# A two-layer kernel: rounded passes for two products, a moved weight product, an earlier Tanh and a moved tile step

## What is computed

```python
xn = layernorm(x)
# layer 0: a small state-space branch and a gated feed-forward with ternary weights
h  = silu(conv(xn @ in_w.T + in_b) + conv_b)
a, b = exp(-exp(xp[:16])), silu(xp[16:]) * h.sum()        # xp = h @ xp_w.T + xp_b
s_t = s_{t-1} * a_t + b_t                                  # scan over the sequence
u  = silu((xn @ w1.T) * w1_s) * ((xn @ w2.T) * w2_s)       # 128 -> 512, twice
u  = gelu((u @ h1.T) * h1_s); u = gelu((u @ h2.T) * h2_s)  # 512 -> 512
x  = x + (s @ out_w.T + out_b) + (u @ w3.T) * w3_s
# layer 1: test-time-training attention, and a mixture of 8 experts (top 2) with a shared expert
xn = layernorm(x)
# attention: 16 heads of 64, chunks of 64 tokens; per chunk
#   Z = K W + b, normalised; gradient of the loss; W -= (eta K)^T grad; out = norm(Q W + b)
# experts: scores = sigmoid(xn @ gate_w.T + gate_b), top 2, y = w2_e(gelu(w1_e x)); shared expert on all tokens
x  = x + attention(xn) @ wo + routed + 0.1 * shared
```

## Time and profile before

| | |
|---|---|
| median of 3 runs | 624.35 us (621.68 to 625.32) |
| the profiled execution | 628.44 us, span 626.6 us |
| mean granted clock of TensorE | 0.965 |
| TensorE busy (matmul / weight load) | 92% / 67% of the span |
| VectorE, ScalarE, GpSimd busy | 77%, 50%, 43% |
| first layer | 0 to about 195 us |
| second layer, chunks of one block | about 98 us for a block |

### The profile page before, as it was taken

One profiled execution on the slowest core, in us unless ns is written; L12 is line 12 of the kernel. 1 busy time (PEld: TensorE's weight loads), 2 busy tenths in 40 slices (PEclk: granted clock), 3 DMA queues, 4 the chain that ended last, 5 costly groups with the idle time before them and its releaser, 6 DMA issues.

```text
span 626.6 us, 14164 instructions
## 1 busy us (share of the span) xinstructions
PE 576.5 (92%) x5515; PEld 418.2 (67%) x5515; DVE 485.3 (77%) x866; ACT 315.0 (50%) x598; POOL 267.8 (43%) x253
## 2 busy tenths in 40 slices
PE   2999999999998979898999999999999989998886
PEld 0477574773774635555778777878778768677576
DVE  2694787995994596898769969877869879779793
ACT  1553566583475614451656456756357566345111
POOL 0933000036066363238241844862744853616422
PEclk9999999998999889896999999999999999999598
DMA  7999300000001010004516115325203423000301
...
DMA packets 37890, 53.15 MB, mean 85 GB/s; under 512 B 10168, under 2 KB 23120, under 8 KB 37440
## 3 DMA queue, kind: packets, MB, share of 16 engines
...
## 4 chain that ended last, share of the span: by engine, by line
PE 69%; DVE 21%; POOL 4%; issue 3%; ACT 2%; DMA 0%; POOLq 0%; SPq 0%; ACTq 0%; DVEq 0%
PE ps L963 10%; PE ps L824 8%; PE ps L1066 7%; PE ps L1029 4%; PE ps L830 4%; PE ps L1132 4%; PE ps L1074 4%; PE ps L1037 4%; POOL small L687 3%; PE ps L989 3%; PE ps L1116 3%; DVE small L1832 2%; PE ps L886 2%; PE ps L936 2%; PE ps L887 2%
## 5 line engine op out<-in xcount | busy, mean ns | idle before, releaser
L687 POOL TENSOR_TENSOR small<-small 128x8 f32<-128x8 f32 x32 | 53.6, 1685 | 109.5 <-DVE small L1770 109.4
L766 POOL TENSOR_TENSOR small<-small 128x8 f32<-128x8 f32 x32 | 52.0, 1641 | 38.2 <-DVE small L1762 38.2
L731 POOL DMA_INDIRECT ys_dram<-ybuf,slot_row x39 | 51.7, 1325 | 12.8 <-issue 8.3
L1386 ACT ACTIVATE sq<-ps 128x512 f32<-128x512 f32 x32 | 19.1, 597 | 66.8 <-PE ps L1066 66.8
L1418 ACT ACTIVATE work<-ps,b1t 128x128 f32<-128x128 f32 x156 | 44.6, 369 | 15.5 <-PE ps L1029 13.3
L1116 PE MATMUL ps<-grad,l 64*64 64x64 f32 x1024 | 32.1, 227 | 13.0 <-DVE grad L1847 12.2
L1762 DVE TENSOR_REDUCE small<-sq 128x8 f32<-128x520 f32 x32 | 22.1, 694 | 27.2 <-ACT sq L1386 26.4
L1377 ACT ACTIVATE x_query<-ps 128x512 f32<-128x512 f32 x32 | 17.5, 594 | 49.7 <-PE ps L989 49.7
L1544 DVE RECIPROCAL got<-got 128x512 f32<-128x512 f32 x8 | 26.8, 3348 | 19.3 <-ACT got L1272 19.3
L1116 PEld LDWEIGHTS ps<-grad,l 64*64 64x64 f32 x1024 | 30.1, 140 | 16.8 <-issue 12.8
L715 POOL DMA_INDIRECT xs_dram<-wtile,pos x32 | 36.3, 1135 | 9.8 <-issue 7.6
...
## 6 DMA issues: line engine op xcount, KB each, us to landing
...
```

The source lines that it names most:

```text
L687: pool.tensor_tensor(small[:, 240 + 8 * p:248 + 8 * p], small[:, 224 + 8 * p:232 + 8 * p], small[:, 384:392], ALU.pow).then_inc(q_r.sem, 1)
L731: pool.indirect_dma_start(ys_dram, bass.IndirectOffsetOnAxis(ap=slot_row[:, k:k + 1], axis=0), ybuf[:, k // 4 % 2, k % 4], None).then_inc( ...
L766: pool.tensor_tensor(small[:, 16 + 8 * p:24 + 8 * p], small[:, 8 * p:8 * p + 8], small[:, 384:392], ALU.pow).then_inc(z_r.sem, 1)
```

## The change

- **w1 and w2 in three rounded passes.** For blocks 1 to 3 each float32 product with `w1` or `w2` becomes three passes on rounded parts. GpSimd splits the two weights into `wt` (free until the target weights fill it), after it has waited for `x_lo`. VectorE splits the normalised block i+1 into `xn_hi` and `xn_lo` in block i. Block 0 stays as it was. `xn_hi` lies in the memory of `sw1`, so the load of `sw1` moves behind block 3's w1 and w2 products.
- **Target weights** move from the end of block 2 to the end of block 3, with ScalarE's copies and VectorE's subtractions; TensorE's wait for them moves ahead of the first target product.
- **Tanh.** A Tanh on two numbers is done after the keys, so that the table is loaded there, and the last gates' Tanh stands ahead of the target copies.
- **Ranks** of the last block stand ahead of all shared products.
- **One tile step** goes from (2,1) to (3,2).

```diff
--- before.py
+++ after.py
@@ -113,6 +113,8 @@
         wq = sb("wq", [P, 2, NH * HD], F32R)
         wk = sb("wk", [P, 2, NH * HD], F32R)
         wt = sb("wt", [P, 2, NH * HD], F32R)
+        with ExitStack() as first_layer:
+            xn_hi = first_layer.enter_context(nc.sbuf_tensor("xn_hi", [P, NB], F32R))
         sw1 = sb("sw1", [P, HID])
         xb_s = sb("xb_s", [P, 2, NB], F32R)
         wo = sb("wo", [P, NQ, D])
@@ -142,6 +144,7 @@
         gb = got[:, 0].rearrange("p k d -> p (k d)")
         xb_t = sb("xb_t", [P, 2, NB], F32R)
         x_less = sb("x_less", [P, NB])
+        xn_lo = sb("xn_lo", [P, NB], F32R)
 
         work = sb("work", [P, 8192])
         used = [0]
@@ -272,7 +275,7 @@
         a_u = signal("a_u", KC)
         a_uh, a_ul = signal("a_uh", KC), signal("a_ul", KC)
         a_gh, a_gl = signal("a_gh", KC), signal("a_gl", KC)
-        h_sp = sem("h_sp")
+        h_sp, x_hi, x_lo = sem("h_sp"), sem("x_hi"), sem("x_lo")
         a_h1 = signal("a_h1", KC)
         a_g1 = signal("a_g1", KC)
         a_h2 = signal("a_h2", KC)
@@ -365,7 +368,7 @@
             take_slot(("out", i, 0), a_res.sem, a_res.at(i, 2))
             if i == 0:
                 take_slot(("prep", 0, 0), p_dve, 3)
-            if i == 2:
+            if i == NBLK - 1:
                 for p in range(2):
                     take_slot(("wt", 0, p), w_t, p + 1)
         slot_no = {k: n for n, (k, _, _) in enumerate(slots)}
@@ -388,7 +391,7 @@
 
         TILES = 4 * QUADS - 1
         STEPS = {(0, 3): 4, (1, 0): 5, (1, 1): 1, (1, 2): 5, (1, 3): 4,
-                 (2, 0): 5, (2, 1): 1, (2, 2): 5, (2, 3): 3, (3, 0): 5, (3, 2): 3}
+                 (2, 0): 5, (2, 2): 5, (2, 3): 3, (3, 0): 5, (3, 2): 4}
         assert sum(STEPS.values()) == TILES + 2
 
         def steps_before(i, c):
@@ -545,12 +548,14 @@
             sp.dma_start(wqT, a["wqT"]).then_inc(ld_c, 16)
             sp.dma_start(wkT, a["wkT"]).then_inc(ld_c, 16)
             sp.dma_start(sw2[:, :, :], a["mw2"][:, EXP * KC:, :]).then_inc(ld_m, 16)
-            sp.dma_start(sw1[:, :], a["mw1"][:, EXP, :]).then_inc(ld_s, 16)
             sp.wait_ge(zeroed, 1)
             sp.dma_start(xs_dram.rearrange("(p t) d -> p (t d)", p=P).rearrange("p (r z) -> p r z", z=ZEROS),
                          zeros.unsqueeze(1).to_broadcast([P, SLOTS // P * ROW // ZEROS, ZEROS])).then_inc(z_st, 16)
 
             for i in range(NBLK):
+                if i == NBLK - 1:
+                    sp.wait_ge(a_w12.sem, a_w12.at(i, KC))
+                    sp.dma_start(sw1[:, :], a["mw1"][:, EXP, :]).then_inc(ld_s, 16)
                 sp.wait_ge(a_res.sem, a_res.at(i, 2))
                 sp.dma_start(x_dram[:, blk(i)], x_sb[:, blk(i)]).then_inc(x_st[i], 16)
             sp.wait_ge(b_ctc, 1)
@@ -661,7 +666,14 @@
                 step(pool.tensor_copy(to[:, 0], src))
                 step(pool.tensor_tensor(to[:, 1], src, to[:, 0], ALU.subtract))
 
-            pool.wait_ge(a_gl.sem, a_gl.at(0, KC))
+            pool.wait_ge(ld_a, 6 * 16)
+            pool.wait_ge(x_lo, 1)
+            for n, w in enumerate((w1, w2)):
+                at = slice(n * HID, (n + 1) * HID)
+                pool.tensor_copy(wt[:, 0, at], w).then_inc(h_sp, 1)
+                parts[0] += 2
+                pool.wait_ge(h_sp, parts[0] - 1)
+                pool.tensor_tensor(wt[:, 1, at], w, wt[:, 0, at], ALU.subtract).then_inc(h_sp, 1)
             step(pool.tensor_tensor(wv_f, wk_f, wv_f, ALU.subtract))
             step(pool.tensor_tensor(gb[:, :], gg[:, :], gb[:, :], ALU.mult))
             step(pool.tensor_tensor(heads_of(wkv_f), wv_f.rearrange("p (q h d) -> p h q d", h=2, d=HD), heads_of(gg[:, :]),
@@ -882,10 +894,20 @@
                 for m in range(DC):
                     pe.matmul(open_slot("in", i, m), in_w[:, m * P:(m + 1) * P], xn[:, blk(i)],
                               start=True, stop=True).then_inc(a_in.sem, 1)
+                if i:
+                    pe.wait_ge(x_lo, i)
+                    pe.wait_ge(h_sp, 4 * KC + 4)
                 for m in range(KC):
-                    pe.matmul(open_slot("w1", i, m), w1[:, m * P:(m + 1) * P], xn[:, blk(i)], start=True, stop=True)
-                    pe.matmul(open_slot("w2", i, m), w2[:, m * P:(m + 1) * P], xn[:, blk(i)],
-                              start=True, stop=True).then_inc(a_w12.sem, 1)
+                    for n, (kind, w) in enumerate((("w1", w1), ("w2", w2))):
+                        to = open_slot(kind, i, m)
+                        if i:
+                            at = slice(n * HID + m * P, n * HID + (m + 1) * P)
+                            pe.matmul(to, wt[:, 0, at], xn_hi[:, :], start=True, stop=False)
+                            pe.matmul(to, wt[:, 1, at], xn_hi[:, :], start=False, stop=False)
+                            mm = pe.matmul(to, wt[:, 0, at], xn_lo[:, :], start=False, stop=True)
+                        else:
+                            mm = pe.matmul(to, w[:, m * P:(m + 1) * P], xn[:, blk(i)], start=True, stop=True)
+                    mm.then_inc(a_w12.sem, 1)
                 centre(*ahead_of[0])
                 if i >= 2:
                     pe.wait_ge(ln_out.sem, ln_out.at(norm_no[1, i - 2], 1))
@@ -940,13 +962,11 @@
                 pe.matmul(to, out_w, ssm[0:NST, 4], start=True, stop=True).then_inc(a_o.sem, 1)
                 if i == 0:
                     folded_weights()
-                if i == 2:
+                if i == NBLK - 1:
                     target_weights()
 
             pe.wait_ge(p_dve, PREP)
             pe.wait_ge(p_pool, P_LATE)
-            pe.wait_ge(w_t, 2)
-
 
             def free(kind, i, which):
                 n = ring_no[kind, i, which]
@@ -1165,6 +1185,7 @@
             pe.wait_ge(ln_out.sem, ln_out.at(norm_no[1, NBLK - 1], 1))
             pe.wait_ge(*last_slot[3])
             gates(bank(3), NT - JB, NT)
+            pe.wait_ge(w_t, 2)
             project_targets(0, 0)
             tokens_turned(free("x", NBLK - 1, 0), NBLK - 1).then_inc(r_pe, 1)
 
@@ -1186,9 +1207,8 @@
                 tiles(steps_of(i, 0, 0, 3))
                 project_targets(i, 1)
                 if i == 0:
-                    shared_up(0, 0, 1)
                     ranks(NBLK - 1, bank(2), 0)
-                    shared_up(0, 1, KC)
+                    shared_up(0)
                     shared_up(1, 0, 2)
                     shared_down(0)
                     shared_up(1, 2, KC)
@@ -1464,9 +1484,10 @@
             keys_in(0, 1, 3)
             spread_in(1, NBLK - 1)
             keys_in(0, 3, NQ)
+            act.activation(small[:, 100:102], eps_ln, ACT.Tanh)
             key_squares(0, 0)
+            gates_in(NBLK - 1)
             targets_in(0, 0)
-            gates_in(NBLK - 1)
             tokens_out(take("x", NBLK - 1, 0), NBLK - 1).then_inc(r_act, 1)
             for i in range(NBLK):
                 keys_by_token(i, 0)
@@ -1699,6 +1720,11 @@
                         less_hi(i, m - 1, a_gh, a_gl)
                 less_hi(i, KC - 1, a_gh, a_gl)
                 normalised(*ahead_of[0])
+                if i < NBLK - 1:
+                    dve.wait_ge(ln_out.sem, ln_out.at(norm_no[ahead_of[0]], 1))
+                    dve.tensor_copy(xn_hi[:, :], xn[:, blk(i + 1)]).then_inc(x_hi, 1)
+                    dve.wait_ge(x_hi, i + 1)
+                    tt(xn_lo[:, :], xn[:, blk(i + 1)], xn_hi[:, :], ALU.subtract).then_inc(x_lo, 1)
                 if i >= 2:
                     places(i - 2, slot_bank("rank", i - 2, 0), 0)
                 if i == NBLK - 1:
```

## The result

The changed kernel takes 616.66 us (median of 4, 613.75 to 617.28), the kernel before beside it 624.83: a ratio of 0.9872, 95% interval 0.9823 to 0.9921. It is faster by 8.2 us, more than the 5.1 forecast, and inside the range. A second set, taken with the later experiments, gave 0.9837 (0.9733 to 0.9940). The profiled execution took 616.73 us with a span of 614.9, against 628.44 and 626.6.

A forecast was written before the change was run, and what follows sets the result against it. The prediction took TensorE (69% of the chain of waits), then VectorE (21%), and TensorE's half-rate clock as bounds. Terms -2.3 + 1.1 + 0.4 - 1.9 - 0.5 - 1.9 = -5.1 us took 624.35 to 619.3, range 614.5 to 624.5.

The forecast's parts named there:

- Passes: w1 and w2 products, blocks 1 to 3: gains of 1.37, 0.9 and nothing, together -2.3 us.
- one such meeting: Block 3: a VectorE subtraction meeting GpSimd's token splitting costs up to 1.3 us, eating the 1.37 gain.
- GpSimd in block 0: Block 0: GpSimd's later weight splitting delays VectorE's scans, so TensorE gets the state output 1.1 us late; +1.1 us.
- the stepping in turns: Block 0: VectorE and GpSimd instructions taken alternately, second scan ending at 56.4, state output 1.1 us late.
- Target weights: Moved behind block 3: half-rate stretch follows to the key projections, square-root table load some 0.4 us late; +0.4 us.
- Tanh and ranks: Second layer's start: early Tanh and ranks before shared products bring the gradients forward by 1.04 + 0.86; -1.9 us.
- Step out of (2,1): Chunk (2,1): removing a 2.0 us tile step gives only -0.5 us, as turned queries then wait for ScalarE.
- Step into (3,2): Chunk (3,2): the added step fills TensorE's 3.51 us pause, so updates run at full rate; -1.9 us.
- Of the rivals, the first: Half rate retreats further, before 230 and at block 3's start, 1.6 us each: 617.7 or 616.1; chance 0.17.
- The second: VectorE takes the passes' gain and (3,2) stays at half rate: 623.5; chance of both 0.1, of one 0.2.
- The third: Slower: new short waits bring half rate into the first layer, 1.6 us per stretch, 628.9; chance 0.05.
- The fourth: The change doesn't do what it says: the Tanh table load could be issued twice; chance under 0.02.

The follow-up runs named there:

- A second set: The changed kernel, unedited, measured and profiled again beside the later experiments: 621.00 us against 629.56 for the kernel before, ratio 0.9837.
- before's second profile: The kernel before, with no edit, profiled once more: 627.66 us, span 625.8.

## Why the prediction was right, and where not

- **Passes, -2.3.** Right: 2.7 us by stages at like clock. Block 1 gave 1.30 (1.37), block 2 0.81 (0.9), block 3 0.55 (0.4 to 0.8 over the profiles) where the step said nothing; "one such meeting, up to 1.3 us, eats the 1.37" took the meeting at its upper bound, and the rows show 0.48.
- **GpSimd in block 0, +1.1.** Mis-sized: 0. From the first `in_w` product to the state output of block 0 it takes 39.35 us in the changed kernel and 39.36 in before's second profile; over all profiles it is 39.0 to 40.6 us with either code, and TensorE nowhere waits for the state output. The step that failed is the stepping in turns: it had GpSimd through its four short instructions by 51.5 and put the 2.4 us ones opposite the scans. They were held by VectorE themselves and ran to 53.67, so the scans met a cast and a subtraction, and ended at 54.2, not 56.4. The Trainium skill's rule (SBUF — State Buffer, "Who interferes with whom") is not at fault: the rows show both stretched, VectorE's and GpSimd's. The use of it here was.
- **Target weights, +0.4.** Mis-sized, and for a wrong reason. The move costs nothing (99.23 against 99.20 us). "I assume that the half-rate stretch follows its instructions" failed: it followed in one of eight profiles with the moved order fully and in two by 1.3 us. Behind block 2 and up to the key state, four of six profiles of the old order had 1.7 to 5 us of it. Over the profiles at hand, with the 1.36 us of the passes in blocks 2 and 3 added back, the mean is 101.3 us for the old order (99.2 to 104.2) and 100.2 for the new (99.0 to 103.8), so I put the term at -1.1, and in the pair of first profiles it is over -2. With such a spread six and eight profiles do not show that it differs from 0.
- **Tanh and ranks, -1.9.** Right in kind, a bit small: 2.45, of which 1.46 is the Tanh and 0.98 the ranks. The sum of the held TensorE (1.04) and a product (0.86) left out that the ranks' input itself was late. The hoped-for full clock behind 230 did not come: the pause of 3.27 us was still enough for a half-rate stretch.
- **Step out of (2,1), -0.5.** Mis-sized: up to 0.8 in two stages, up to 0.7 given back in (3,0): about -0.1, and over (2,1) to (3,2) whole nothing that can be told. What came late next was (3,0), which the step did not name.
- **Step into (3,2), -1.9.** (Its own numbers, 591.6 - 589.8, give 1.8.) Right in mechanism, shown twice, by the real step and by products that do nothing. The stage gives 1.8 us and the last stage gives 0.6 back in the first profiles; over all profiles it is 2.2 (45.8 against 43.6), since without it the half rate can run on into the last stage (22.77 us at a clock of 0.67 in before's second profile).

By the runs the terms sum to -2.7 + 0 - 1.1 - 2.45 - 0.1 - 2.2 = -8.6 us, against 8.2 measured on medians. The nearness is in part luck, since -1.1 and -2.2 are means over stretches that come and go, and the interval of the measured ratio alone leaves 4.9 to 11.1 us. The 3.1 us that the forecast missed are mostly three terms: 1.1 for GpSimd that never came, 0.4 and -1.1 for the target weights, and 0.55 for the ranks and the Tanh.

Of the rivals, the first was half right: the half rate retreated, but at block 3's start and in the last stages, and not before the first updates. The second fell in both halves. The third, the half rate in the first layer, "so far TensorE has no pause between 62 and 148 and stays at full clock", rested on one execution: the stretch at 60 to 68 us is in eleven of the fourteen profiles, whole or in part, with either code, and so no effect of the change; the first of before is one of the three without it, the changed kernel's second another. The fourth fell: both Tanh and Gelu loads stand where the order put them.

The changed profile against the first one of before shows 11.7 us of span, 3.5 more than the medians. All of that surplus lies in (2,1) to (3,2): 148.4 us in before's first profile against 145.8 to 146.5 in six others with the old `STEPS`, and 143.9 in the changed kernel's first against 146.5 in its second, none of them with a half-rate stretch but in their last 1.2 us. (The profile of the changed kernel without the step has such a stretch in (2,3), and 151.7 us.) What made that stretch long in the one and short in the other wasn't settled.
